# A post-LN decoder layer on one core: maximum pass in row-half pairs, shifts and self sums turned by VectorE, LayerNorm scaling on GpSimd, and a new order

## What is computed

```python
qkv = hidden_states @ Wqkv; q, k, v = jnp.split(qkv, 3, axis=-1)
q, k = rope(rmsnorm(q, q_norm_w)), rope(rmsnorm(k, k_norm_w))     # in heads
x = _layernorm(x + softmax(mask(q k^T * scale)) v @ Wo)
qh = x.reshape(b * 8, 16, 512); kh = vh = ctx.reshape(b * 8, 16, 512)
qk = jnp.einsum('bdm,bdn->bmn', qh, kh) * scale
x = _layernorm(x + jnp.einsum('bmn,bcn->bcm', softmax(qk), vh))
x = _layernorm(x + _quant_dequant(x) @ _quant_dequant(weight).T)
```

## Time and profile before

| | |
|---|---|
| runs | 3355.9 us median of 3 (3354.95 to 3358.13) |
| span of the profiled execution | 3353.3 us |
| mean granted TensorE clock | 0.982 |
| instructions | 79176 |
| transfers | 220.66 MB, 66 GB/s |
| PE, DVE, ACT, POOL busy | 3148.0, 2792.0, 2093.1, 1251.8 us |

### The profile page before, as it was taken

How to read it: one execution, slowest core, us unless ns; L and a number is a source line. 1 busy time by engine, 2 the same in 40 slices (tenths; PEclk the granted TensorE clock), 3 DMA queues, 4 the chain that set the end, 5 groups by cost and what they waited for, 6 DMA issues and landing times.

```text
span 3353.3 us, 79176 instructions
## 1 busy us (share of the span) xinstructions
PE 3148.0 (94%) x22224; PEld 1676.5 (50%) x22224; DVE 2792.0 (83%) x5187; ACT 2093.1 (62%) x3905; POOL 1251.8 (37%) x1623
## 2 busy tenths in 40 slices
PE   1689999999999999999999999999999999999986
PEld 1445555555555555555555555555555555555432
DVE  6368888888888888888888888888888888888874
ACT  0346666666676666666667666666666766666653
POOL 3223334334343333433433333343343433334321
PEclk9789999999999999999999999999999999999997
DMA  2022222222222222222222122222222222222220
GB/s 75 26 62 74 71 67 71 63 72 65 70 73 64 72 64 66 71 63 73 64 70 73 63 71 66 66 71 63 71 66 70 73 63 71 65 66 71 67 64 17
DMA packets 203973, 220.66 MB, mean 66 GB/s; under 512 B 37760, under 2 KB 160640, under 8 KB 203776
## 3 DMA queue, kind: packets, MB, share of 16 engines
q1 hardware_dynamic: 203776, 218.77, 21.4%
...
## 4 chain that ended last, share of the span: by engine, by line
PE 75%; DVE 14%; issue 7%; POOL 2%; ACT 1%; DVEq 1%; DMA 1%; SPq 0%; POOLq 0%; ACTq 0%
PE bank L872 19%; PE mx L985 14%; PE st L1002 13%; PE pv L1014 12%; PE bank L865 5%; PE bank L907 3%; DVE nm L715 3%; PE bank L956 3%; DVE st L776 2%; PE bank L939 2%; PE bank L959 2%; DVE lin_l L743 1%; DVE yout L838 1%; PE bank L923 1%; PE bank L920 1%
## 5 line engine op out<-in xcount | busy, mean ns | idle before, releaser
L715 DVE TENSOR_REDUCE nm<-mx 128x1 f32<-128x512 f32 x2048 | 1355.0, 685 | 219.9 <-PE mx L985 210.2
L559 ACT ACTIVATE pp<-st 128x512 f32<-128x512 f32 x2048 | 1153.0, 597 | 400.9 <-PE st L1002 385.1
L985 PE MATMUL mx<-kst,qst 96*128 96x512 bf16 x2048 | 765.4, 387 | 29.2 <-DVE nm L715 28.8
L1002 PE MATMUL st<-qst,kst 98*128 98x512 f16 x2048 | 739.6, 387 | 6.9 <-DMA qst<-cross_shift 2.6
L1014 PE MATMUL pv<-pp,vT 128*32 128x512 f32 x4096 | 551.2, 610 | 0.0
L985 PEld LDWEIGHTS mx<-kst,qst 96*128 96x128 f16 x2048 | 189.1, 98 | 445.5 <-DVE nm L715 283.1
L872 PE MATMUL bank<-w_h,lin_h 128*128 128x512 f32 x768 | 394.0, 513 | 4.5 <-DVE lin_l L743 4.4
L1002 PEld LDWEIGHTS st<-qst,kst 98*128 98x128 bf16 x2048 | 190.7, 98 | 317.8 <-ACT pp L559 216.6
L490 POOL TENSOR_SCALAR rstd<-mv 128x1 f32<-128x1 f32 x192 | 36.9, 192 | 817.2 <-DVE mv L779 812.1
L872 PE MATMUL bank<-w_l,lin_h 128*128 128x512 f32 x768 | 306.0, 398 | 0.0
L872 PE MATMUL bank<-w_h,lin_l 128*128 128x512 f32 x768 | 305.0, 397 | 0.0
...
## 6 DMA issues: line engine op xcount, KB each, us to landing
...
```

Of the source, the lines that this page charges most:

```text
L559: a.activation(pp[:, unit % 2, j, :], st[n % 2][:], ACT.Exp, scale=CROSS_SCALE).then_inc(st_free, 1)
L715: v.tensor_reduce(nm2[:, n // 16, n % 16:n % 16 + 1], mx[n % 2][:], AX.X, ALU.max, negate=True)\
L985: t.matmul(mx[n % 2][:], qst[b.i][0:XROWS, h, c * P:(c + 1) * P], kst[b.i][0:XROWS, h, :], start=True, stop=True).then_inc(mx_full, 1)
L1002: t.matmul(st[n % 2][:], kst[b.i][:, h, i * P:(i + 1) * P], qst[b.i][:, h, :], start=True, stop=True).then_inc(st_full, 1)
```

## The change

1. The maximum pass works on pairs of heads. Two tiles of their own, qpair and kpair, hold one head of a pair on partitions 0 to 63 and the other on 64 to 127, each as four planes of 16 rows (before: five planes and a zero one, 96 rows; the product of the low q plane with the second k plane is left out of the maximum). `cross_scores` issues two matmuls of 64 rows into the two banks of one tile mx; `cross_max` reduces both at once; 16 of each a batch in place of 32. The tiles are loaded by `ld_kpair` and `ld_qpair`, eight transfers a half each.
2. The shifts are turned by VectorE in blocks of 32x32 and stored so; the loads put them in order in pieces of 64 bytes. The TensorE transposes and ScalarE copies go.
3. The self sums go to one block of 128 columns (sums_of puts each part's sums on its own rows), which VectorE turns, inverts once in 16 columns, and turns back spread.
4. `layernorm` and `oT_low` run on GpSimd.
5. Each of the three kinds of linear input has its own operand tiles. qst and kst have one buffer instead of two.
6. All tables of steps and the bank table are new. Their rows are not shown; the places below show what they make.

```diff
@@ -45,15 +45,19 @@
     XROWS = 96
 
     Q_PLANE, K_PLANE = (0, 0, 0, 1, 1), (0, 1, 2, 0, 1)
+    Q_PAIR, K_PAIR = (0, 1, 0, 0), (0, 0, 1, 2)
+    ROW_TILE, PAIRS = 64, XH // 2
+    PG = PAIRS // GROUPS
     N_SC = XH * KC
+    N_MX = PAIRS * KC
...
-    sh1_d = nc.dram_tensor("self_shift", [BATCH, 2 * NH, TOK], F16, kind="Internal").ap()
-    sh2_d = nc.dram_tensor("cross_shift", [BATCH, GROUPS, 32, P], F16, kind="Internal").ap()
+    sh1_d = nc.dram_tensor("self_shift", [BATCH, TOK, 2 * NH], F16, kind="Internal").ap()
+    sh2_d = nc.dram_tensor("cross_shift", [BATCH, GROUPS, P, 32], F16, kind="Internal").ap()
...
-        lin_h, lin_l = sb("lin_h", [P, D], F32R), sb("lin_l", [P, D], F32R)
+        xT_h, xT_l = sb("xT_h", [P, D], F32R), sb("xT_l", [P, D], F32R)
+        oT_h, oT_l = sb("oT_h", [P, D], F32R), sb("oT_l", [P, D], F32R)
+        xdT_h, xdT_l = sb("xdT_h", [P, D], F32R), sb("xdT_l", [P, D], F32R)
...
-        ones = sb("ones", [P, HD])
+        sums_of = sb("sums_of", [P, KC, HD])
...
-        qst = [sb(f"qst{i}", [XROWS + 2, XH, D], F16) for i in range(2)]
-        kst = [sb(f"kst{i}", [XROWS + 2, XH, D], BF16) for i in range(2)]
+        qst = sb("qst", [XROWS + 2, XH, D], F16)
+        kst = sb("kst", [XROWS + 2, XH, D], BF16)
+        qpair = sb("qpair", [P, PAIRS, D], F16)
+        kpair = sb("kpair", [P, PAIRS, D], BF16)
...
-        mx = [bank(f"mx{i}") for i in range(2)]
+        mx = es.enter_context(nc.psum_tensor("mx", [P, 2, 512], F32))
...
-            ld_cx:0@2 ld_qst:1@3 ld_kst:0@3 ld_x:0@0 st_sh2:1@4 ld_sh2:1@4 st_out:0@5 st_qpl:0@2
...
+            st_x2:0@4 st_kpl:0@4 ld_sh1:0@3 ld_kst:0@5 st_qpl:0@4 st_sh2:0@5 ld_sh2:0@5
...
+            def ld_kpair(b, g):
+                sp.wait_ge(d_kpl_stored, b.n(16, 16))
+                sp.sem_inc(passed_sp, 1)
+                sp.wait_ge(mx_full, b.n(N_MX, N_MX // GROUPS * (g + 1) - N_MX))
+                sp.sem_inc(passed_sp, 1)
+                for q in range(2):
+                    for r in range(4):
+                        row = ROW_TILE * q + r * XD
+                        sp.dma_start(kpair[row:row + XD, PG * g:PG * (g + 1), :],
+                                     kpl_d[b.idx()][K_PAIR[r]].rearrange("(p q d) n -> q d p n", q=2, d=XD)
+                                     [q][:, PG * g:PG * (g + 1), :]).then_inc(d_kpair[g], 16)
+
+            def ld_qpair(b, g):
+                sp.wait_ge(d_qpl_stored, b.n(16, 16))
+                sp.sem_inc(passed_sp, 1)
+                sp.wait_ge(mx_full, b.n(N_MX, N_MX // GROUPS * (g + 1) - N_MX))
+                sp.sem_inc(passed_sp, 1)
+                for q in range(2):
+                    for r in range(4):
+                        row = ROW_TILE * q + r * XD
+                        sp.dma_start(qpair[row:row + XD, PG * g:PG * (g + 1), :],
+                                     qpl_d[b.idx()][Q_PAIR[r]].rearrange("(p q d) n -> q d p n", q=2, d=XD)
+                                     [q][:, PG * g:PG * (g + 1), :]).then_inc(d_qpair[g], 16)
...
-                sp.wait_ge(st_full, b.n(N_SC, N_SC // GROUPS * (g + 1) - 2 * N_SC))
+                sp.wait_ge(st_full, b.n(N_SC, N_SC // GROUPS * (g + 1) - N_SC))
...
-                sp.dma_start(qs[SROWS:SROWS + 2, :, :],
-                             sh1_d[b.idx()].rearrange("(a h) q -> a h q", a=2)).then_inc(d_sh1, 16)
+                for a in range(2):
+                    sp.dma_start(qs[SROWS + a:SROWS + a + 1, :, :].rearrange("a h (u y) -> a h u y", y=32),
+                                 sh1_d[b.idx()].rearrange("(u a h) y -> a h u y", a=2, h=NH)[a:a + 1]).then_inc(d_sh1, 16)
...
-                sp.dma_start(qst[b.i][XROWS:XROWS + 2, GH * g:GH * (g + 1), :]
-                             .rearrange("a h (c m) -> a (h c) m", c=KC),
-                             sh2_d[b.idx()][g].rearrange("(a r) m -> a r m", a=2)).then_inc(d_sh2[g], 16)
+                sp.wait_ge(st_full, b.n(N_SC, N_SC // GROUPS * (g + 1) - N_SC))
+                sp.sem_inc(passed_sp, 1)
+                for a in range(2):
+                    sp.dma_start(qst[XROWS + a:XROWS + a + 1, GH * g:GH * (g + 1), :]
+                                 .rearrange("a h (c u y) -> a (h c) u y", c=KC, y=32),
+                                 sh2_d[b.idx()][g].rearrange("(u a r) y -> a r u y", a=2, r=16)[a:a + 1]).then_inc(d_sh2[g], 16)
...
+            def layernorm(b, i):
+                rows = (x2, x3, yout)[i]
+                pool.wait_ge(s_rstd[i], b.n(1, 1))
+                pool.sem_inc(passed_pool, 1)
+                g_.tensor_scalar(rows[:], rows[:], mv[i][:, 0:1], rstd[i][:], ALU.subtract, ALU.mult)\
+                  .then_inc(s_ln[i], 1)
...
+            def oT_low(b, _):
+                pool.wait_ge(s_oTh, b.n(1, 1))
+                g_.tensor_tensor(oT_l[:], o1[:], oT_h[:].bitcast(F32), ALU.subtract).then_inc(s_oTl, 1)
...
-            def cross_shift_out(b, g):
-                act.wait_ge(*full(f"mT{g}", b))
-                act.wait_ge(d_sh2_stored[g], b.n(16, 0))
-                a.activation(sh2T[g][:], at(f"mT{g}")[0:32, 0:P // 2].bitcast(F16), ACT.Copy)\
-                 .then_inc(bank_free[BANK[f"mT{g}"]], 1)
...
             def cross_max(b, n):
-                dve.wait_ge(mx_full, b.n(N_SC, n + 1))
-                v.tensor_reduce(nm2[:, n // 16, n % 16:n % 16 + 1], mx[n % 2][:], AX.X, ALU.max, negate=True)\
-                 .then_inc(mx_free, 1)
+                dve.wait_ge(mx_full, b.n(N_MX, n + 1))
+                p, c = n // KC, n % KC
+                cols = nm2[:, p // PG, :].rearrange("m (l q c) -> m l q c", l=PG, q=2)[:, p % PG, :, c]
+                v.tensor_reduce(cols, mx[:], AX.X, ALU.max, negate=True).then_inc(mx_free, 1)
 
             def cross_shift(b, g):
 
-                dve.wait_ge(mx_free, b.n(N_SC, 16 * (g + 1)))
-                v.tensor_scalar(nm2[:, g, :], nm2[:, g, :], 1.0 / SHIFT_UNIT, None, ALU.mult).then_inc(s_sc2, 1)
-                dve.wait_ge(s_sc2, b.n(GROUPS, g + 1))
-                v.tensor_copy(sh2[:, g, 0, :], nm2[:, g, :]).then_inc(s_h2, 1)
+                dve.wait_ge(mx_free, b.n(N_MX, N_MX // GROUPS * (g + 1)))
+                v.tensor_scalar(sh2[:, g, 0, :], nm2[:, g, :], 1.0 / SHIFT_UNIT, None, ALU.mult).then_inc(s_h2, 1)
                 dve.wait_ge(s_h2, b.n(GROUPS, g + 1))
-                v.tensor_tensor(sh2[:, g, 1, :], nm2[:, g, :], sh2[:, g, 0, :], ALU.subtract).then_inc(s_sh2, 1)
+                v.scalar_tensor_tensor(sh2[:, g, 1, :], nm2[:, g, :], 1.0 / SHIFT_UNIT, sh2[:, g, 0, :],
+                                       ALU.mult, ALU.subtract).then_inc(s_l2, 1)
+                dve.wait_ge(s_l2, b.n(GROUPS, g + 1))
+                dve.wait_ge(d_sh2_stored[g], b.n(16, 0))
+                v.transpose(sh2T[g][:], sh2[:, g].rearrange("p a r -> p (a r)")).then_inc(s_sh2[g], 1)
...
-            def self_recip(b, c):
-
+            def self_recip(b, _):
                 dve.wait_ge(*full("pvs", b))
-                cols = slice(c * P, (c + 1) * P)
-                done = s_r1 if c < KC - 1 else bank_free[BANK["pvs"]]
-                v.reciprocal(o1[:, cols], at("pvs")[:, cols]).then_inc(done, 1)
+                v.transpose(sumT[:].rearrange("p u c i -> p (u c i)"), at("pvs")[:, 0:P])\
+                 .then_inc(bank_free[BANK["pvs"]], 1)
+                dve.wait_ge(*freed("pvs", b))
+                v.reciprocal(r1[:].unsqueeze(3), sumT[:, :, :, 0:1]).then_inc(s_r1, 1)
+                dve.wait_ge(s_r1, b.n(1, 1))
+                dve.wait_ge(s_oTl, b.n(1, 0))
+                v.transpose(o1[:].rearrange("p (c u y) -> p c u y", c=KC, u=KC),
+                            r1[:].rearrange("p u c -> p c u").unsqueeze(3).to_broadcast([P, KC, KC, HD]))\
+                 .then_inc(s_r1T, 1)
 
             def self_norm(b, _):
                 dve.wait_ge(*full("pvo", b))
-                dve.wait_ge(s_r1, b.n(KC - 1, KC - 1))
-                dve.wait_ge(*freed("pvs", b))
+                dve.wait_ge(s_r1T, b.n(1, 1))
                 v.tensor_tensor(o1[:], at("pvo")[:], o1[:], ALU.mult).then_inc(bank_free[BANK["pvo"]], 1)
...
-            def layernorm(b, i):
-                rows = (x2, x3, yout)[i]
-                dve.wait_ge(s_rstd[i], b.n(1, 1))
-                v.tensor_scalar(rows[:], rows[:], mv[i][:, 0:1], rstd[i][:], ALU.subtract, ALU.mult)\
-                 .then_inc(s_ln[i], 1)
...
-                    last = t.matmul(at("pvs")[HD * j:HD * (j + 1), cols], ones[:], p1[c % 2][:, j, :],
-                                    start=True, stop=True)
+                    last = t.matmul(at("pvs")[HD * j:HD * (j + 1), 0:P], sums_of[:, c, :], p1[c % 2][:, j, :],
+                                    start=(c == 0), stop=(c == KC - 1))
...
-                h, c = n // KC, n % KC
-                if n % (GH * KC) == 0:
-                    pe.wait_ge(d_kst[b.i][h // GH], b.n2(80, 80))
-                    pe.wait_ge(d_qst[b.i][h // GH], b.n2(80, 80))
-                pe.wait_ge(mx_free, b.n(N_SC, n - 1))
```

(24 more changed lines are left out.)

211 lines of the change are left out of this document (101 added, 110 removed), and 6 rows, old and new, of the table BANK.

## The result

The changed kernel takes 3159.8 us (median of four runs, 3158.94 to 3167.57) beside 3355.4 for the kernel before on the same chip: a ratio of 0.942, with an interval of 0.941 to 0.944. The forecast was 3248; the measured time lies under its main range (3190 to 3300) and inside its range for 8 in 10 (3090 to 3390). The profiled execution has a span of 3157.2 us, 196 less than before.

What follows compares the result with a forecast made beforehand. TensorE's steady-state sequence was taken as the bound: 46.2 + 0.35 + 1.1 = 47.6 us a slot against 49.3, 1.7 x 64 = 108 us less, so 3248 us; range 3190 to 3300 (60%), 8 in 10 3090 to 3390.

Steps and rivals of the forecast that it cites:

- borders: TensorE's changes between array layouts: about 0.104 us each, 48 a slot in the new order where 28 were before.
- The price of a pair: Maximum pass on TensorE: 0.217 + 0.05 for an unhidden second weight load + 0.21 for both borders, 0.48 us.
- Slot: One batch's work on TensorE: 46.2 us plus 0.35 and 1.1 of waits, 47.6 us against 49.3.
- Waits: TensorE's idle time a slot: 2.3 us before; 0.35 at the loop's turn and 1.1 scattered kept.
- VectorE's share of the turn: TensorE's wait at the loop's turn, put down to late maxima: 0.7 us a slot, half should vanish.
- Filling and emptying: Time outside the full slots: left as it is, some 200 us, plus or minus 25.
- Shift rows: Shift transposes leave TensorE: at most 0.8 us a slot of its work goes, and a 0.5 us wait.
- GpSimd's scaling: LayerNorm scalings moved to GpSimd: 1.16 us each, with oT_low 4.6 us more a slot, covered by idle time.
- VectorE: Reductions, self sums, scalings and oT_low: some 8 of 42.7 us a slot go, busy near 75%; by itself worth nothing.
- 14 us over: SyncE's queue: 68 transfers a slot instead of 33, 33 us of issue in 47, so it fits.
- Rival (3): SyncE becomes the bound if its waits exceed 15 us a slot; slot 50 or more, 3400 us; chance 10%.
- Own operand buffers: Separate operand tiles for linear layers: cost nothing, gain nothing; a small gain or loss lies within the range.

Runs made afterwards that it cites:

- the moved kernel: The changed kernel with 64 increments of an unused semaphore on ScalarE ahead of its loop, nothing in the loop touched: 3121.7 us, ratio 0.932.
- the placed experiment: The changed kernel with the three LayerNorm scalings back on VectorE, standing later, and GpSimd computing each deviation earlier: 3161.7 us, ratio 0.942.

## Why the prediction was right, and where it was off

The direction held: TensorE's slot bounds both kernels and is shorter, and the scalings on GpSimd are cover. The forecast said 108 us less, and 196 came. Of the 2.4 us a slot the runs show two parts alone: the shift rows 0.8, and row halves against two full matmuls 0.4. The other 1.2, half of the gain, no run takes apart; in them lie one reduction for two heads, the turned self sums, the own buffers and the new order. The forecast's own sum had nothing for the pairs: 32 matmuls at 0.217 are 6.9 us, and 16 pairs with 26 more borders 7.0; its 1.7 us were 0.8 of shift rows and 0.85 of waits.

- *The price of a pair* is the term that was mis-sized most. Forecast 0.267 us and 0.21 of borders; measured 0.217 and 0.20. The second weight load that I added is hidden. At 16 pairs, 0.8 us a slot, 51 us. The borders held: rows of the array pay what columns paid in the earlier trace rows. The Trainium skill, "TensorEngine Tiling (Array Packing)", Key Properties, says that a change of the tiling mode drains the engine; the trace shows a cost for it, 0.09 and 0.11 us. The Trainium skill, "TensorE: Matmul & The Clock Gate", Part 3, gives a pack the time of one matmul and some ns; the trace agrees for the pair's own work, 0.217 us.
- *Slot* 47.6 forecast, 46.9 measured: 46 us, the 51 of the pairs less a little more waiting.
- *Waits* were forecast as 0.35 + 1.1 = 1.45 us a slot and measured as 1.5 (46.9 less 45.4, which is the forecast's 46.2 with the 0.8 of the pairs taken off), but the parts are other ones. I halved VectorE's share of the turn. In the moved kernel no slot is longer than another, so VectorE's part is wholly gone from TensorE's path. In its place came 0.8 us a slot of ScalarE's turn, a new wait that no row of before showed, for there q14 had 5 packets a turn and not 10. The other 0.7 us are scattered; 0.4 of them are 0.11 each at four places of a slot where a linear part stands directly behind a pair or a P·V unit. The right sum was luck.
- *Filling and emptying* "as they are" was wrong by 42 us, the rest of the difference (108 + 46 + 42 = 196). The first x transpose is 5 us earlier, the eleven distances behind it take 448 instead of 497 us (26 of these 49 are the shorter slot), and from the last transpose to the end are 207 instead of 225 us. In the early windows TensorE's clock is higher too (columns of the earlier trace rows; of before, then of after):

```profile
110.00:160.00 50.00, 32.71 (x275) 23.60 (x273) 18.34 (x31) 18.55 (x32) 19.07 (x24) 0.80 0.13 41
160.00:210.00 50.00, 36.53 (x236) 23.92 (x237) 29.66 (x51) 17.06 (x29) 13.00 (x17) 0.80 0.19 57
```

```profile
110.00:160.00 50.00, 38.51 (x285) 26.37 (x286) 24.76 (x41) 20.07 (x33) 24.69 (x28) 0.97 0.23 67
160.00:210.00 50.00, 45.25 (x322) 23.73 (x320) 37.97 (x56) 31.29 (x58) 20.21 (x24) 0.97 0.35 105
```

  Before, TensorE ran between its levels (0.80 of 2.4 GHz) while it was busy 33 and 37 of 50 us; now it is busy 39 and 45 of 50 at 0.97. How much of the 42 us is the clock and how much the other order of the stages stays open: no run took them apart.
- *Shift rows*: forecast 0.8 us of TensorE and the 0.5 us wait; alone they gave 0.8 in all. In that kernel TensorE takes 0.31 and 0.15 us more than their work behind two turned scores a little later, so most of the wait moved instead of going.
- *GpSimd's scaling* was off (2.08 for 1.16) at no cost, as the placed experiment shows. *VectorE* came out within 0.15 us for each operation, the largest the first one of the self shift (0.32 for 0.17). But its busy time fell from 42.8 to 37.5 us a slot, 5.3 and not 8, and is 80% in the steady state, not 75. The forecast took sums of means from a busy time in which neighbours overlap (the means of the kernel before add up to 3021 us, its busy time is 2792), and had nothing for the shift operations, which take 0.45 us a slot more. As VectorE isn't the bound, neither moved the time.
- *SyncE*: "14 us over" was too much. Some 4 us are left, by the estimate above. Rival (3) was nearer than its 10% said, though its price was right in kind: sixteen issues more, and it is there.
- *Own operand buffers*, at nothing, weren't tried alone, nor were pairs or turned self sums in the kernel before: what each is worth stays open.
